# A two-layer block on one core: units of one sequence in place of pairs, network weights resident, and every wide dense product as three float32r products of high and low parts

## What is computed

```python
x = x + layernorm(attn_block(layernorm(x)))
x = x + layernorm(ffn(layernorm(x)))

# attn_block, on xm = a layer norm of x, scaled by channel
n = rms_norm(xm); vg = n @ in_proj_w                    # 128 -> 512
value = silu(causal_conv4(vg[..., :256])); gate = vg[..., 256:]
Bm, Cm = xm @ B_proj_w, xm @ C_proj_w                   # 128 -> 1024 each, 16 heads of 64
y = selective_scan(value, A, Bm, Cm, dt)                # per head (C B^T * decay mask) @ value
xm += ((y + D * value) * silu(gate)) @ out_proj_w
xm += relu(rms_norm(xm) @ m_fc_w)**2 @ m_proj_w         # 128 -> 512 -> 128
q, k, v = rms_norm(xa) @ (q_w, k_w, v_w)                # 16 heads of 8, 4 key heads
xa += softmax(causal(rope(rms_norm(q)) @ rope(rms_norm(k)).T)) @ v @ o_w
xa += relu(rms_norm(xa) @ a_fc_w)**2 @ a_proj_w

# ffn, scales by output channel left out
h = silu(x @ w1) * (x @ w2)                             # 128 -> 512
h = gelu(h @ h1); h = gelu(h @ h2)                      # 512 -> 512, twice
return h @ w3                                           # 512 -> 128
```

## Time and profile before

| | |
|---|---|
| time, median of 3 runs | 1063.42 us (1061.19 to 1063.50) |
| the profiled execution, its own time | 1061.02 us |
| its span | 1059.3 us |
| mean granted TensorE clock, of full speed | 0.965 |
| busy: TensorE | 949.9 us, 90% |
| busy: VectorE | 650.2 us, 61% |
| busy: ScalarE | 527.2 us, 50% |
| busy: GpSimd | 251.5 us, 24% |
| chain that ended last | TensorE 66%, VectorE 8%, ScalarE 3% |
| DMA | 32.51 MB, 30 GB/s over the span |

### The profile page before, as it was taken

One profiled execution on the slowest core, in us unless ns is written; L12 is line 12 of the kernel. 1 busy time (PEld: TensorE's weight loads), 2 busy tenths in 40 slices (PEclk: granted clock), 3 DMA queues, 4 the chain that ended last, 5 costly groups with the idle time before them and its releaser, 6 DMA issues.

```text
span 1059.3 us, 18517 instructions
## 1 busy us (share of the span) xinstructions
PE 949.9 (90%) x7008; PEld 585.2 (55%) x7008; DVE 650.2 (61%) x1715; ACT 527.2 (50%) x1123; POOL 251.5 (24%) x410
## 2 busy tenths in 40 slices
PE   1678688698999999999999999999999999689787
PEld 0455454564565756576666656575656655544433
DVE  4955886596676656776686657766667634831311
ACT  3424437546662566437572667247552662273131
POOL 3001104222330423114310523023300511160200
PEclk9899899899999999999999999999999999689989
DMA  7000000000111011110111001101011011002110
GB/s 223 1 1 1 11 2 1 11 2 11 31 31 51 12 30 31 41 31 11 31 40 41 21 21 31 56 16 31 11 41 32 21 40 50 21 11 63 46 43 27
DMA packets 52311, 32.51 MB, mean 31 GB/s; under 512 B 2688, under 2 KB 49024, under 8 KB 52224
## 3 DMA queue, kind: packets, MB, share of 16 engines
q1 hardware_dynamic: 52224, 31.33, 10.1%
HBM read 29.23 MB, written 2.10 MB: 30 GB/s over the span
## 4 chain that ended last, share of the span: by engine, by line
PE 66%; DVE 8%; ACT 3%; issue 1%; POOL 1%; POOLq 0%; DVEq 0%; ACTq 0%
PE bank L1147 54%; PE CB L1147 7%; DVE cv L900 2%; PE bank L1158 2%; DVE mneg L1053 1%; PE bank L1388 1%; PE bank L1346 1%; DVE cv L896 1%; ACT xpad L641 1%; ACT junk L595 1%; PE bank L1302 1%; ACT bnT L602 0%; ACT val L632 0%; POOL relu L522 0%; DVE bn L849 0%
## 5 line engine op out<-in xcount | busy, mean ns | idle before, releaser
L1053 DVE TENSOR_REDUCE mneg<-bank 128x2 f32<-128x512 f32 (+1 forms) x192 | 119.4, 685 | 43.5 <-PE bank L1147 43.4
L914 DVE TENSOR_TENSOR M<-CB,LM 128x512 f32<-128x512 f32 x128 | 87.8, 686 | 87.8 <-PE CB L1147 87.0
L1147 PE MATMUL bank<-hC,slot 128*128 128x512 f32 x256 | 115.6, 599 | 0.0
L1147 PE MATMUL bank<-hD,slot 128*128 128x512 f32 x256 | 114.2, 592 | 0.0
L602 ACT ACTIVATE relu<-bank 128x512 f32<-128x512 f32 x64 | 38.8, 606 | 84.8 <-PE bank L1147 84.3
L1147 PEld LDWEIGHTS bank<-hC,slot 128*128 128x128 f32 x256 | 46.9, 190 | 51.7 <-issue 50.7
L1147 PEld LDWEIGHTS bank<-hD,slot 128*128 128x128 f32 x256 | 47.5, 190 | 50.2 <-issue 49.3
L497 POOL TENSOR_TENSOR oms<-omv,eps_ln 128x4 f32<-128x4 f32 x8 | 1.6, 199 | 286.0 <-DVE omv L843 286.0
L752 ACT ACTIVATE hD<-bank,cols 128x512 f32<-128x512 f32 x32 | 22.0, 688 | 91.9 <-PE bank L1147 91.9
L1147 PE MATMUL CB<-cv,relu 64*128 64x256 f32 (+1 forms) x512 | 59.1, 349 | 6.9 <-DVE M L915 6.8
L1147 PE MATMUL CB<-ct,relu 64*128 64x256 f32 (+1 forms) x512 | 59.8, 352 | 5.7 <-DVE M L915 5.7
(11 more groups left out here) (224 smaller groups left out, 2016.1 us busy)
## 6 DMA issues: line engine op xcount, KB each, us to landing
slot<-in_w_h SPq DMA_DIRECT2D x64, 256.0 KB, 3.0
slot<-in_w SPq DMA_DIRECT2D x16, 256.0 KB, 2.6
xh<-in_x SPq DMA_DIRECT2D x8, 256.0 KB, 2.9
x_res<-in_x SPq DMA_DIRECT2D x8, 256.0 KB, 2.9
out<-out_sb SPq DMA_DIRECT2D x8, 256.0 KB, 2.3
relu<-in_w_B SPq DMA_DIRECT2D x1, 512.0 KB, 5.1
relu<-in_w_C SPq DMA_DIRECT2D x1, 512.0 KB, 5.7
PX<-in_rows SPq DMA_DIRECT2D x1, 320.0 KB, 6.0
```

The source lines that it names most:

```text
L914: v.tensor_tensor(both(M[:, k % 2, r, :, 0:2 * P]), both(CB[:, :, 0:2 * P]), first, ALU.mult)
L1053: v.reduce_max(neg, of, axis=AX.X, negate=True).then_inc(evac("K", n), 1)
L1147: return p.matmul(o, lhsT, rhs, start=start, stop=True, skip_group_check=True)
```

## The change

A unit is one sequence of 256 tokens; there are 16. All tiles of tokens are half as wide. The banks of PSUM stay 512 wide, and where two blocks of 256 are made, they share a bank and are often evacuated by one instruction (`gates`, `bc` with B and C side by side, `up`, `up_b`); silu and gelu of the last network take 256 columns each, since their scale differs by block.

Every product of `gates`, `up`, `up_b`, `gate` (the old `gate1` and `gate2` together) and `hidden` is now a `split_product` of 256 columns. That needs low and high parts of the weights, made once at the start (`w_first`, `w_mix`, `w_back`, `w_ffn`), and of the tokens. For the transposed tiles (n, n2, n4, x2, as xm before) ScalarE writes the high part (`hi_part`) and VectorE the low part (`lo_part`). For the hidden layers' inputs ScalarE copies the high part from SBUF and GpSimd subtracts (`hd_part`, `hc_part`, two of 512 columns each); `hidden1` and `hidden2` wait for both.

The weights of the last network, high and low, stay in SBUF; the slots, `stream` and its waits are gone. Their float32 form is loaded once into tiles that attention uses later, and the first `wt` waits until it has been split.

The scaling of the four rms norms is on ScalarE in place of VectorE. There are three buffers for `xh` in place of two, four for `xa` in place of two, two for `x1`, `xmT` and `Vr` in place of one; `yacc_free` of the scan and of the network are separate. `TURNS` and `BANKS` are new; five units are in work at a time in the repeated part.

The diff, cut to its core:

```diff
-PAIRS = BATCH // 2
-TOK = 2 * L
+UNITS = BATCH
+TOK = L
...
+XBUF = 3
+ABUF = 4
...
-    slot = [sb(f"slot{b}", [P, NBLK, P]) for b in range(SLOTS)]
+    w_1_hi, w_1_lo = sb("w_1_hi", [P, HID], F32R), sb("w_1_lo", [P, HID], F32R)
+    w_2_hi, w_2_lo = sb("w_2_hi", [P, HID], F32R), sb("w_2_lo", [P, HID], F32R)
+    w_h1_hi, w_h1_lo = sb("w_h1_hi", [P, NBLK, HID], F32R), sb("w_h1_lo", [P, NBLK, HID], F32R)
+    w_h2_hi, w_h2_lo = sb("w_h2_hi", [P, NBLK, HID], F32R), sb("w_h2_lo", [P, NBLK, HID], F32R)
...
+    xh = [sb(f"xh{b}", [P, TILES, D]) for b in range(XBUF)]
...
+    xa = [sb(f"xa{b}", [P, TILES, D]) for b in range(ABUF)]
...
-        def stream(i, n):
-            g = i * STREAM + n
-            if g >= SLOTS:
-                wait_read(sp, g - SLOTS)
-            sp.dma_start(slot[g % SLOTS][:], streamed(n)).then_inc(S[f"slot{g % SLOTS}"], 16)
...
+        def w_ffn(i, _):
+            pool.wait_ge(ffn_hi, 1)
+            for w, hi, lo in ffn_split:
+                last = g.tensor_tensor(lo[:], w, hi[:].bitcast(F32), ALU.subtract)
+            last.then_inc(ffn_lo, 1)
+            pool.wait_ge(ffn_lo, 1)
+            g.memset(Qs[:], 0.0).then_inc(ffn_lo, 1)
+
+        def hd_part(i, b):
+            two = slice(2 * b, 2 * b + 2)
+            pool.wait_ge(S["hd_hi"], at(i, "hd_hi", b + 1))
+            g.tensor_tensor(hD_lo[:, two, :], h[:, two, :], hD_hi[:, two, :].bitcast(F32), ALU.subtract).then_inc(S["hd_lo"], 1)
+
+        def hc_part(i, b):
+            two = slice(2 * b, 2 * b + 2)
+            pool.wait_ge(S["hc_hi"], at(i, "hc_hi", b + 1))
+            g.tensor_tensor(hD_lo[:, two, :], h[:, two, :], hD_hi[:, two, :].bitcast(F32), ALU.subtract).then_inc(S["hc_lo"], 1)
...
+        def rms_norm(src, dst, r):
+
+            for k in range(TILES):
+                last = a.activation(dst[:, k, :], src[:, k, :], ACT.Copy, scale=r[:, k:k + 1])
+            return last
...
+        def n4(i, _):
+            if i > 0:
+                wait_full(act, "F", i - 1, F_X2)
+            act.wait_ge(S["rs_b"], 3 * i + 1)
+            rms_norm(xa[i % ABUF], bn, brs).then_inc(S["nrm_b"], 1)
+
+        def hd_part(i, b):
+            two = slice(2 * b, 2 * b + 2)
+            wait_evac(act, "F", i, F_W + 2 * b + 1)
+            a.activation(hD_hi[:, two, :], h[:, two, :], ACT.Copy).then_inc(S["hd_hi"], 1)
+
+        def hi_part(c, i, n, dst, done):
+
+            wait_full(act, c, i, n)
+            a.activation(dst, psum_t(c, i, n), ACT.Copy).then_inc(S[done], 1)
+
...
+        def hc_part(i, b):
+            two = slice(2 * b, 2 * b + 2)
+            wait_full(act, "F", i, F_H1 + 1)
+            wait_evac(act, "F", i, F_H1 + b)
+            a.activation(hD_hi[:, two, :], h[:, two, :], ACT.Copy).then_inc(S["hc_hi"], 1)
...
+        def lo_part(c, i, n, hi, lo, done):
+
+            dve.wait_ge(S[done], i + 1)
+            v.tensor_tensor(lo, psum_t(c, i, n), hi.bitcast(F32), ALU.subtract).then_inc(evac(c, n), 1)
...
-        def split_product(o, w_hi, w_lo, x_hi, x_lo):
-
-            mm(o, w_hi, x_hi, True)
+        def split_product(o, w_hi, w_lo, x_hi, x_lo, start):
+
+            mm(o, w_hi, x_hi, start)
             mm(o, w_hi, x_lo, False)
...
-        def project(c, i, n, w, src):
+        def block(o, b):
+            return o[:, b * TOK:(b + 1) * TOK]
+
+        def project(c, i, n, w_hi, w_lo, b, x_hi, x_lo):
 
             wait_free(pe, c, i, n)
-            mm(psum(c, i, n), w, src, True).then_inc(full(c), 1)
+            for k in range(2):
+                j = slice((2 * b + k) * P, (2 * b + k + 1) * P)
+                last = split_product(block(psum(c, i, n), k), w_hi[:, j], w_lo[:, j], x_hi[:], x_lo[:], k == 0)
+            last.then_inc(full(c), 1)
 
...
+            wait_free(pe, "F", i, F_W + j)
+            J = slice(j * P, (j + 1) * P)
+            o = psum("F", i, F_W + j)
+            split_product(block(o, 0), w_1_hi[:, J], w_1_lo[:, J], x2T_hi[:], x2T_lo[:], True)
+            split_product(block(o, 1), w_2_hi[:, J], w_2_lo[:, J], x2T_hi[:], x2T_lo[:], False).then_inc(full("F"), 1)
...
+        def hidden(i, n, b, w_hi, w_lo, x_hi, x_lo):
+            wait_free(pe, "F", i, n + b)
+            for k in range(2):
+                J = slice((2 * b + k) * P, (2 * b + k + 1) * P)
+                for c in range(NBLK):
+                    last = split_product(block(psum("F", i, n + b), k), w_hi[:, c, J], w_lo[:, c, J], x_hi[:, c, :], x_lo[:, c, :], k + c == 0)
             last.then_inc(full("F"), 1)
```

More of the change, by code:

```diff
@@ L104, in _chains @@
-    tail = [("load_res", 0), ("y_turn", 0), ("o_proj", 0), ("o_sq", 0), ("n4", 0), ("n4_turn", 0)] + several("up_b", NBLK)
-    tail += several("down_b", NBLK) + [("res_b", 0), ("ln_a", 0), ("ln_a2", 0), ("ln_b", 0)]
-    ffn = [("x2_turn", 0)]
-    for j in range(NBLK):
-        ffn += [("gate1", j), ("gate2", j)]
-    ffn += several("hidden1", NBLK) + several("hidden2", NBLK) + several("ffn_out", NBLK)
-    ffn += [("f_stats", 0), ("f_norm", 0), ("store", 0)]
-    stream = several("stream", STREAM)
@@ new lines, in _chains @@
+    attention = [("v_in", 0), ("k_turn", 0)] + several("q2_turn", TILES) + piece(0) + piece(1) + [("pv", 0)] + piece(2) + [("pv", 1)]
+    attention += several("y_rows", 2)
+    tail = [("load_res", 0), ("y_turn", 0), ("o_proj", 0), ("o_sq", 0), ("n4", 0), ("n4_turn", 0)] + several("up_b", 2)
+    tail += several("down_b", 2) + [("res_b", 0), ("ln_a", 0), ("ln_a2", 0), ("ln_b", 0)]
+    ffn = [("x2_turn", 0)] + several("gate", NBLK) + several("hd_part", 2) + several("hidden1", 2) + several("hc_part", 2) + several("hidden2", 2)
@@ L180, in _opened @@
-        y_rows=["A", A_YT(k)], y_turn=["T", T_Y], o_proj=["B", 0], n4_turn=["T", T_N4], up_b=["T", T_FC + k],
-        down_b=["B", 1] if k == 0 else [], x2_turn=["F", N_X2], gate1=["F", N_W + 2 * k], gate2=["F", N_W + 2 * k + 1],
-        hidden1=["F", N_H1 + k], hidden2=["F", N_H2 + k], ffn_out=["FO", 0] if k == 0 else []).get(name, [])
+        xm_turn=["M", M_XM], n_turn=["M", M_N], gates=["M", M_G + k], val_turn=["M", M_XT], bc=["S", k],
+        va=["Y", 0] if k == 0 else [], m_out=["D", D_O] if k == 0 else [], n2_turn=["D", D_N2], up=["D", D_FC + k],
@@ new lines, in _opened @@
+        down=["Y", 1] if k == 0 else [], n3_turn=["H", H_N3], qkv=["H", H_QKV], qk_turn=["K", K_Q + k], k_turn=["A", A_K],
+        scores=["K"] + [K_S + HKV * k + j for j in range(HKV)], q2_turn=["A", A_TURN + k], wts=["A"] + [A_EXP + HKV * k + j for j in range(HKV)], pv=["PV", k],
+        y_rows=["A", A_YT + k], y_turn=["T", T_Y], o_proj=["B", 0], n4_turn=["T", T_N4], up_b=["T", T_FC + k],
+        down_b=["B", 1] if k == 0 else [], x2_turn=["F", F_X2], gate=["F", F_W + k],
+        hidden1=["F", F_H1 + k], hidden2=["F", F_H2 + k], ffn_out=["FO", 0] if k == 0 else []).get(name, [])
```

994 lines of the change are left out of this document (489 added, 505 removed).

## The result

The changed kernel takes 1054.72 us (median of 8 runs, 1050.82 to 1059.03); the kernel before, in the same comparison, 1063.46. The ratio is 0.9928, 95% interval 0.9904 to 0.9951. That is 0.8% faster where 3.5% was forecast. The profiled execution has a span of 1056.4 us and a mean granted clock of 0.959; its own time, 1058.08, is 3.4 above the median (over the eight runs the clock is 0.957 to 0.969).

What follows compares the result with a forecast made beforehand. The prediction took TensorE to bound the middle, the rest being ramp. 16 x 58.2 = 931, plus ramp 90, plus 2 for starting work, gave a span of 1023 and a forecast of 1026 us, 3.5% faster; range 968 to 1088.

Steps and rivals of the forecast that it cites:

- The products: TensorE's wide products, now float32r of 256 columns: 0.12 us each, bounds 0.107 and 0.232; TensorE's work 55.1 a unit.
- The other engines: Busy time a unit: ScalarE 42.3 us, VectorE 43.9, GpSimd about 25.
- The period: Repeated middle part: 58.2 us a unit, against 58.25 for half a pair before.
- the walk: One repeated unit followed through each engine's written order: TensorE late at six places, 3.1 us of stalls in sum.
- what the products give, the chains take back: Middle part: TensorE's saving on products is lost to waits through ScalarE, 58.2 us a unit against 58.25.
- the ScalarE rival: Middle part: evacuations at full durations make ScalarE's chains the limit, 63 to 64 us a unit, 1110 in all; chance 0.15.
- The ramp: Both ends of the span: 127 us falls to 90, bounds 79 and 127; the first 28 stay.
- I take 0.63: 62: Both ends: the 99 us beyond the first 28 scale by 0.63 with a unit's shorter stages, leaving 62.
- TensorE stays the wall: Rival, middle part: TensorE's waits mostly vanish, 55.6 us a unit, 984 in all; chance 0.27.
- The pitch doesn't halve: Rival, wide products: 0.232 us each despite half the columns, 78 a unit, 1342 in all; chance 0.05.
- ScalarE's chains set the pace: Rival, middle part: slower from 60.6 us a unit, 1110 in all, mostly nearer to 1085; chance 0.15.
- The ramp doesn't shrink: Rival, both ends: ramp stays 127 us, its length being in stages, not tokens; 1062, no change; chance 0.08.

Runs made afterwards that it cites:

- e7: Changed kernel with the third product (low weights by high tokens) left out of every wide dense product, 68 products a unit less: 1018.48 us.
- e6: Changed kernel without GpSimd's four low parts of the hidden layers' inputs, products reading the high part instead: 1023.43 us.
- e11: Changed kernel with GpSimd's low-part subtractions for the hidden layers' inputs made copies of one operand at the same places: 1027.50 us.
- e4: Changed kernel with silu and gelu replaced by relu, so no table is loaded between exp, silu and gelu: 1021.25 us.
- e3: Changed kernel with 185 idle float32 products (filler) put where TensorE waits longest in the fill and the drain: 1037.06 us.
- e5: Kernel before with 202 idle products (filler) at 29 waits in the fill and the drain: 1067.19 us, ratio 1.0054.
- e13: Kernel before with 86 idle products (filler) at seven of its longest waits: 1065.80 us, ratio 1.0032.
- e8: Changed kernel with idle products in both ends and low parts of the last two units' hidden inputs on VectorE: 1034.43 us.

## Why the prediction was right or wrong

**The products: right.** Taken 0.12, measured 0.118, and the same in e7. TensorE's work a unit: 55.1 forecast, 55.2 measured. The instruction count rose by 2048.

**The other engines: right in size.** ScalarE 42.3 forecast, 42.2 measured; VectorE 43.9 and 44.3; GpSimd 25 and 22.5. The 99 table loads are there. VectorE's figure is right by luck: without GpSimd's subtractions it is 42.4 (e6), so the sum was 1.5 too high, and the disturbance that it left out adds 1.9.

**The period: right in size, half right in reason.** 58.2 forecast and measured; the walk gave 3.1 of stalls and 3.0 are there. The walk has the waits for `hT`, `Kb` and the copy of pv; those it put at o_proj and up_b aren't among the period's waits, and one it hadn't, `n2T_lo` (0.7), is. It comes from the disturbance that the prediction named beside the ScalarE rival and left out of the sum: 1.3 a unit by e6 and e11, some 20 us in all. Without it the period is 56.9, so that the exact 58.2 is in part luck: the walk's stalls were too high by about what the disturbance adds. And "what the products give, the chains take back" is stronger than written: e7 shows that a further 8 us off TensorE is worth 2. The table loads are worth 2.2 a unit (e4).

**The ramp: wrong.** The step that failed is "I take 0.63: 62": of 99 us beyond the first 28, 62 were to be left, and 97 are. The first store was forecast "near 240" and came at 244, so a unit's way through the stages did get shorter by that factor. What was wrong is to apply it to the whole ramp. The ramp is that way less the credit of the drain. The credit is the work already done on the units in flight, less what TensorE idles and loses to the clock while it finishes them, and it fell nearly as the unit did: 113.5 to 61.9 us. The prediction's own first store gives the measured ramp once the credit is halved: 240 - 58.2 - 113.5 / 2 = 125.

Read by idle and clock it is the same. TensorE's idle outside the periods fell from 101 to 83 us (109.4 - 8 x 1.0, and 131.2 - 16 x 3.0). Its busy time beyond whole periods, 8 x 115.5 and then 16 x 55.2, rose from 26 to 42. By stage, the idle time of 38 to 320 us fell from 45.3 to 30.7, near the factor 0.63, but that after 900 rose from 31.4 to 42.3, where the factor wanted 20. And the prediction let the clock's share, its 22, shrink with the rest to 14; by the stretches at the lower level it is 34. Of this, e3 got about 18 us back, and its ramp is 105. Filler got nothing back in the kernel before (e5, e13), which doesn't show that the clock cost nothing there. Of the 15 that are left above the 90, the low parts on GpSimd are up to 10 by e6; e8, where six of them in the last units are moved to VectorE beside the filler, comes to a ramp of 101. The rest isn't traced to a cause. Why TensorE has more work in the stretches at the lower clock than before, no run tests.

**Rivals.** "TensorE stays the wall" is out: 3.0 of stalls, and e7. "The pitch doesn't halve" is out. "ScalarE's chains set the pace" isn't what happened at 58.2, but its limit stands at 56. "The ramp doesn't shrink", 0.08, is the case that came: its span was 1062 with 4 us for starting work and the rest, measured 1056.4. Its mechanism, "its length is in stages, not tokens", isn't what the runs show: the first unit's way did scale, the drain, with the clock in it, took it back. The 0.08 was too little: the one argument against it, fewer tokens a stage, speaks of the fill alone.
